# Gated attention block on one core: the second batch's transposed input by DMA and GpSimd, and the first batch's GELU low parts ahead of quantising W1

## The reference

```python
xn = layernorm(x)
q, k, v = (gelu(xn @ W1 + b1) @ W2 + b2 for each of q, k, v)
scores = tril(q @ k.T / sqrt(256 * 512))
s = layernorm(scores @ v) * ln_w + ln_b
Wq1, Wq2 = quantise(W1), quantise(W2)
h = relu(xn @ Wq1.T + b1)
g = silu(h @ Wq2.T + b2)
out = x + s * g
```

## Time and profile before

| | |
|---|---|
| median of 3 runs | 307.65 us |
| profiled execution, its own time | 307.09 us |
| span of its instructions | 305.4 us |
| PE busy | 299.8 us, 98% |
| VectorE (DVE) busy | 247.6 us, 81% |
| ScalarE (ACT) busy | 222.4 us, 73% |
| GpSimd (POOL) busy | 133.7 us, 44% |
| granted TensorE clock, mean | 0.999 |
| DMA | 19.06 MB, mean 62 GB/s |

### The profile page before, as it was taken

The page is one execution under the profiler, slowest core; times in us unless marked ns, Lnnn a source line. Parts: engine busy times, 40 slices in busy tenths (PEclk is TensorE's granted clock), DMA queues, the critical chain, the costliest instruction groups (busy, mean ns, idle before and its releaser), DMA issues.

```text
span 305.4 us, 5730 instructions
## 1 busy us (share of the span) xinstructions
PE 299.8 (98%) x1856; PEld 268.7 (88%) x1856; DVE 247.6 (81%) x546; ACT 222.4 (73%) x429; POOL 133.7 (44%) x105
## 2 busy tenths in 40 slices
PE   8999999999999999999999999999999999999995
PEld 7878899889988899888997889888998889988895
DVE  4989798967999589976999669995799858696686
ACT  3696948966786857949489576877679494895862
POOL 3945835167060942429151580609515291404200
PEclk9999999999999999999999999999999999999999
DMA  7970044510007000240004200070001500020001
GB/s 235 375 217 2 1 140 137 166 43 2 1 2 206 0 0 0 58 149 0 0 0 143 64 0 0 1 206 1 0 0 32 174 0 0 0 71 2 0 2 69
DMA packets 15228, 19.06 MB, mean 62 GB/s; under 512 B 1776, under 2 KB 12528, under 8 KB 15216
## 3 DMA queue, kind: packets, MB, share of 16 engines
q1 hardware_dynamic: 14656, 18.51, 19.2%
q10 hardware_dynamic: 560, 0.40, 0.4%
HBM read 14.69 MB, written 4.22 MB: 62 GB/s over the span
## 4 chain that ended last, share of the span: by engine, by line
PE 89%; DVE 4%; DMA 3%; SPq 2%; ACT 1%; issue 0%; POOL 0%; DVEq 0%
PE bank L860 87%; DMA x_all<-in_w1t 3%; DVE g L666 1%; SPq L201 1%; DVE gw L780 1%; DVE gw L658 1%; DVE x_all L660 0%; PE bank L974 0%; DVE gw L809 0%; PE bank L975 0%; DVE w1q L611 0%; ACT r_lo L408 0%; PE bank L972 0%; SPq L212 0%; PE bank L844 0%
## 5 line engine op out<-in xcount | busy, mean ns | idle before, releaser
L756 DVE TENSOR_TENSOR r_lo<-bank,r_hi 128x512 fp32r<-128x512 f32 x64 | 44.0, 691 | 34.8 <-ACT bank L471 34.6
L470 ACT ACTIVATE r_hi<-bank,col 128x512 fp32r<-128x512 f32 x64 | 47.0, 734 | 24.6 <-PE bank L860 24.6
L471 ACT ACTIVATE bank<-bank,col 128x512 f32<-128x512 f32 x64 | 45.4, 710 | 0.0
L367 POOL TENSOR_TENSOR o_rstd<-o_var,neg_half 128x2 f32<-128x2 f32 x16 | 11.2, 699 | 76.2 <-ACT o_var L504 76.2
L322 POOL TENSOR_TENSOR y<-y,xn 128x512 f32<-128x512 f32 x12 | 19.7, 1643 | 56.4 <-DMA y<-in_x_t 56.4
L860 PE MATMUL bank<-xT_lo,w1q 128*128 128x512 f32 x128 | 39.5, 390 | 0.0
L860 PE MATMUL bank<-xT_hi,w1q 128*128 128x512 f32 x128 | 39.5, 390 | 0.0
L449 ACT ACTIVATE g<-bank,col 128x512 fp32r<-128x512 f32 x48 | 34.3, 714 | 1.0 <-PE bank L860 0.9
L860 PE MATMUL bank<-w2q,r_lo 128*128 128x256 f32 x256 | 34.6, 278 | 0.0
L860 PE MATMUL bank<-w2q,r_hi 128*128 128x256 f32 x256 | 34.3, 276 | 0.0
L450 ACT ACTIVATE bank<-bank,col 128x512 f32<-128x512 f32 x48 | 33.1, 689 | 0.0
(11 more groups left out here) (150 smaller groups left out, 686.5 us busy)
## 6 DMA issues: line engine op xcount, KB each, us to landing
out<-x_all SPq DMA_DIRECT2D x15, 256.0 KB, 3.1
x_all<-in_x SPq DMA_DIRECT2D x7, 512.0 KB, 3.5
xn<-x_norm_rows SPq DMA_DIRECT2D x6, 512.0 KB, 4.2
y<-in_x_t SPq DMA_DIRECT2D x6, 512.0 KB, 4.8
x_all<-in_w1t SPq DMA_DIRECT2D x2, 512.0 KB, 7.8
x_all<-in_w2t SPq DMA_DIRECT2D x1, 1024.0 KB, 10.4
row<-in_rows SPq DMA_DIRECT2D x1, 512.0 KB, 4.7
x_all<-in_x SPq DMA_DIRECT2D x1, 256.0 KB, 3.2
```

Source lines behind the costliest of these rows:

```text
L367: nc.gpsimd.tensor_tensor(o_rstd[:, half], o_var[:, half], neg_half[:, half], ALU.pow).then_inc(o_rstd_made, 1)
L470: nc.scalar.activation(r["hi"][:, f], pre[:], ACT.Relu, bias=b1)
L471: nc.scalar.activation(pre[:], pre[:], ACT.Relu, bias=b1).then_inc(f1_whole, 1)
L756: nc.vector.tensor_tensor(r["lo"][:, f], bank[(AT_F1 + f) % BANKS][:], r["hi"][:, f].bitcast(FP32), ALU.subtract).then_inc(r_split, 1)
```

## The change

Batch 1's transposed input is made as that of the later batches. SP's queue issues `load_xT(1)` and `spread_x_norm(1)` right behind the bias rows and before the loads of x 2 and x 3; the wait on `x_norm_stored` is now for the batch's own store. `xn1_tile`, the two tiles on VectorE and the eight transposes are gone. GpSimd's part of batch 0 has a new order: the parts of e first, then the bias row, both `xT_centre`, `quantise_rest` and both `xT_scale`. It starts when all six `g_lo` are made, and `quantise_rest` waits for VectorE's third flags pass in place of the finished `quantise2`. VectorE makes `g_lo` 2 to 5 ahead of `quantise1(0)`; `thresholds(0)` stands between `g_lo` 3 and 4, and `thresholds(1)` behind `quantise1(1)`. ScalarE and VectorE make batch 1's xT parts at the place of the later batches, behind the score parts.

```diff
             def batch(i, first=False, second_last=False, last=False):
                 if first:
-                    pool.wait_ge(x_rstd_made, 1)
-                    pool.wait_ge(xT_summed, 2 * CK)
-                    pool.wait_ge(w1_quantized, 1)
-                    xn1_tile(0)
-                    xn1_tile(1)
-                    pool.wait_ge(v_shift_made, CK + 1)
-                    nc.gpsimd.tensor_scalar(row[:, ROW_B2V], row[:, ROW_B2V], v_shift[:, CK:CK + 1], None,
-                                            ALU.add).then_inc(v_centred, 1)
+                    pool.wait_ge(g_split, 6)
                     pool.wait_ge(e_made, 1)
...
-                    pool.wait_ge(w2_quantized, 1)
+                    pool.wait_ge(v_shift_made, CK + 1)
+                    nc.gpsimd.tensor_scalar(row[:, ROW_B2V], row[:, ROW_B2V], v_shift[:, CK:CK + 1], None,
+                                            ALU.add).then_inc(v_centred, 1)
+                    pool.wait_ge(xT_loaded, 16)
+                    pool.wait_ge(x_norm_loaded, 16)
+                    for k in range(CK):
+                        xT_centre(k)
+                    pool.wait_ge(flags_made, 3)
                     quantise_rest()
+                    for k in range(CK):
+                        xT_scale(1, k)
...
@@ vector engine
+                g_lo(2)
+                g_lo(3)
                 if first:
                     thresholds(0)
+                g_lo(4)
+                g_lo(5)
+                if first:
                     dve.wait_ge(thr_made, 2)
                     quantise1(0)
-                g_lo(2)
-                g_lo(3)
-                g_lo(4)
-                g_lo(5)
-                if first:
                     dve.wait_ge(w1_quantized, 1)
                     quantise1(1)
+                    thresholds(1)
                     dve.wait_ge(w1_quantized, 2)
...
                 if first:
-                    thresholds(1)
                     dve.wait_ge(e_split, 1)
                     quantise2()
...
@@ sync engine
+            load_xT(1)
+            sp.wait_ge(xT_summed, 2 * CK)
+            spread_x_norm(1)
             for b in range(2, RAW1):
                 sp.wait_ge(x_loaded, 16 * b - 16)
                 load_x(b)
...
@@ tensor engine
-                if first:
-                    pe.wait_ge(s_read, TT)
-                    pe.wait_ge(y_read, 1)
-                    transpose_x(xn1_made, [(AT_X1 + k) % BANKS for k in range(CK)], range(TT))
                 ffn_out(i, AT_Y2, (3,), begun=last)
```

More of the change, by code:

```diff
@@ L27 @@
 ORDER = (2, 3, 0, 1, 4, 5)
-AT_X0, AT_X1 = ((2, 3), (4, 6)), 30
+AT_X0 = ((2, 3), (4, 6))
 S_COLS = [T - j * P for j in range(TT)]
@@ L149, in gated_block @@
         x1_stats_made = sem("x1_stats_made")
-        b2q_beside, wq_hi_made, wq_split, wv_hi_made, wv_split, bias_read, xn1_made = (
+        b2q_beside, wq_hi_made, wq_split, wv_hi_made, wv_split, bias_read = (
             sem("b2q_beside"), sem("wq_hi_made"), sem("wq_split"), sem("wv_hi_made"), sem("wv_split"),
-            sem("bias_read"), sem("xn1_made"))
+            sem("bias_read"))
         less_made, more_made, w2_rest_quantized = sem("less_made"), sem("more_made"), sem("w2_rest_quantized")
@@ L223, in spread_x_norm @@
                 sp.dma_start(x_norm_rows[b], x_norm[:]).then_inc(x_norm_stored, 16)
-                sp.wait_ge(x_norm_stored, 16 * b - 16)
+                sp.wait_ge(x_norm_stored, 16 * b)
                 sp.dma_start(x_norm_all, x_norm_rows[b].rearrange("(o p) n t -> o (p n t)", o=1).broadcast_to((P, 2 * T))
                              ).then_inc(x_norm_loaded, 16)
+            load_xT(1)
+            sp.wait_ge(xT_summed, 2 * CK)
+            spread_x_norm(1)
             for b in range(2, RAW1):
@@ L242, in store @@
                              x_all[:, b, t:t + tiles]).then_inc(stored, 16)
-            sp.wait_ge(xT_summed, 3 * CK)
             with sp.Fori(1, B - 1) as i:
@@ L302, in _ @@
                                     ALU.subtract).then_inc(w2v_split, 1)
-            def xn1_tile(t):
-                nc.gpsimd.tensor_scalar(xn[:, t], x_all[:, 1, t], x_mean[:, t:t + 1], x_rstd[:, t:t + 1],
-                                        ALU.subtract, ALU.mult).then_inc(xn1_made, 1)
             def quantise_rest():
@@ L326, in xT_scale @@
                 half = xT32[:, k].rearrange("q (t p) -> q t p", t=TT)
-                pool.wait_ge(xT_centred, CK * (b - 2) + k + 1)
+                pool.wait_ge(xT_centred, CK * (b - 1) + k + 1)
                 nc.gpsimd.tensor_tensor(half, half, x_rstd_all, ALU.mult).then_inc(xT_normalised, 1)
@@ L344, in batch @@
                                             ALU.subtract).then_inc(e_split, 1)
-                    pool.wait_ge(w2_quantized, 1)
+                    pool.wait_ge(v_shift_made, CK + 1)
[6 more added lines that the diff above has]
+                    pool.wait_ge(flags_made, 3)
                     quantise_rest()
+                    for k in range(CK):
+                        xT_scale(1, k)
                 elif not last:
-                    pool.wait_ge(xT_loaded, 16 * i)
-                    pool.wait_ge(x_norm_loaded, 16 * i)
+                    pool.wait_ge(xT_loaded, 16 * i + 16)
+                    pool.wait_ge(x_norm_loaded, 16 * i + 16)
                     for k in range(CK):
@@ L424, in xT_hi @@
                 for k in range(CK):
-                    act.wait_ge(xT_normalised, CK * (b - 2) + k + 1)
+                    act.wait_ge(xT_normalised, CK * (b - 1) + k + 1)
                     nc.scalar.copy(xT["hi"][:, k], xT32[:, k]).then_inc(xT_hi_made, 1)
@@ L488, in batch @@
                     nc.scalar.copy(s["hi"][:, at], s32[:, at]).then_inc(s_hi_made, 1)
-                if not (first or last):
+                if not last:
                     xT_hi(i + 1)
@@ L516, in batch @@
                 squares(1)
-                if first:
-                    for k in range(CK):
-                        act.wait_ge(xT_summed, 2 * CK + k + 1)
-                        nc.scalar.copy(xT["hi"][:, k], bank[(AT_X1 + k) % BANKS][:]).then_inc(xT_hi_made, 1)
                 if not last:
@@ L569, in x_statistics @@
                     return
-                dve.wait_ge(xn1_made, TT)
-                dve.wait_ge(x_norm_stored, 16 * b - 32)
+                dve.wait_ge(x_norm_stored, 16 * b - 16)
                 for t in range(TT):
@@ L704, in batch @@
                 if first:
+                    dve.wait_ge(thr_made, 2)
+                    quantise1(0)
                     dve.wait_ge(w1_quantized, 1)
                     quantise1(1)
+                    thresholds(1)
                     dve.wait_ge(w1_quantized, 2)
@@ L791, in batch @@
                 if not last:
-                    if not first:
-                        xT_lo(i + 1, [xT32[:, k] for k in range(CK)])
-                        dve.wait_ge(xT_split, 2 * i + CK + 4)
+                    xT_lo(i + 1, [xT32[:, k] for k in range(CK)])
+                    dve.wait_ge(xT_split, 2 * i + CK + 4)
                     y_bias(AT_Y0, 0, 2, 3 * i + 1)
@@ L799, in batch @@
                     o_scale(0)
-                    if first:
-                        xT_lo(1, [bank[(AT_X1 + k) % BANKS][:] for k in range(CK)])
                     y_bias(AT_Y2, 3, 1, 3 * i + 3)
```

2 lines of the change are left out of this document (removed).

## The result

The changed kernel takes 309.93 us, the median of 4 runs (309.22 to 310.64), against 307.7 us in 4 runs of the kernel before on the same chip (307.64 to 307.9). The ratio is 1.0067, 95% interval 1.0046 to 1.0088: slower, and inside the forecast's range. A second measurement of the same code gave 309.77 us (6 runs), ratio 1.0051 [1.0034, 1.0068].

What follows compares the result with a forecast made beforehand. TensorE, busy 98% of the span, was taken as the bound. V -0.8, Y0 +1.85, O +0.85, transposes -0.87, batch 1 +0.6 gave +1.6 us: 307.09 to 308.7 profiled, 309.25 as median; range 305.9 to 310.3.

Steps and rivals of the forecast that it cites:

- Transposes: Step 1, TensorE in batch 0: the eight transposes go, all on the path, a gain of 0.87 us.
- V: Step 2, V of batch 0: starts at 22.5 instead of 23.29 us without its wait, gain 0.8 us.
- Exclusion: Step 3, VectorE against GpSimd in batch 0: passes wait for each other, Y0 starts at 38.8, 1.05 us later than before.
- the short hold of the `tensor_scalar`: Within step 3: a GpSimd `tensor_scalar` lets go of VectorE's two-input pass about 0.3 us after it gets in.
- O: Step 4, O of batch 0: waits for GpSimd's low part of v, starts at 45.1, 1.9 us later than before.
- Batch 1: Step 5, start of batch 1: O's 1.9 us less the transposes' 0.87, so 1.03 us late.
- Wait at V: Step 6, V of batch 1: `g_lo` end at 62.0, V is wanted at 61.4, another 0.6 us lost.
- the uncertain holds: Bounds in batch 0: `tensor_scalar` holds of 0.3 us or all of it, the latter +0.5 us.
- the whole gain: Rival for batch 0: passes keep quiet lengths, Y0 and O just in time, -0.8 - 0.87, 306.0 us; chance 0.15.
- full holds: Rival: GpSimd's `tensor_scalar` passes shut out VectorE's L611 to their end, all behind 0.5 us later, 309.8 us; chance 0.15.
- late transfers: Rival: mean and 1/std reach GpSimd at 28 instead of 26.6 us, all behind 0.4 later, 309.7 us; chance 0.06.
- About no change: Rival: GpSimd gets in first behind flags 2 with a short hold, no wait in batch 1, 307.5 us; chance 0.14.

## Why the prediction was right, step by step

The forecast was 1.6 us over before; the medians say 2.2 and 1.8, the starts of V of batch 1 say 1.5 in both traces. By its steps, with the times of the second trace (0.2 earlier as a whole):

| step | forecast | measured |
|---|---|---|
| 2: V of batch 0, no wait | 22.5 | 22.28 |
| 3: e_lo ends | 25.3 | 25.08 |
| 3: second quantising pass ends | 27.2 | 27.05 |
| 3: third flags pass ends | 30.95 | 30.81 |
| 3: last piece of W2 ends, Y0 | 38.8 | 38.66, 38.91 |
| 4: low part of v ends, O | 45.05, 45.1 | 44.96, 45.01 |
| 6: V of batch 1 | 61.95 | 61.64, after a wait of 0.25 |

1. **Transposes.** The gain of 0.87 is there: from O, 1.8 behind before, to the start of batch 1 (50.33, against the 49.4 of before) the lag shrinks by it.
2. **V.** Right in both traces.
3. **Exclusion.** Right to 0.1 us once the start is taken off. That VectorE would get in first behind the third flags pass was right too, and so was the short hold of the `tensor_scalar`: with a hold to its end, the second quantising pass would have ended 0.5 later. What this step left out is D: it waits 0.54 us for an `r_lo`. It costs nothing, since Y0 waits for GpSimd anyway.
4. **O.** Right; the pass that waited longest is the 128x128 multiply, 2.10 us.
5. **Batch 1.** 0.95 late at its start, 1.2 with the earlier start of this execution counted; the sum had 1.03.
6. **Wait at V.** The forecast was 0.6; the traces list 0.25 and none. By the starts, V follows the pair ahead of it by 0.87 and 0.68 us in place of 0.45, so 0.4 and 0.2 us are lost. The term was too large: `g_lo` ends at 59.04 + 2.48 = 61.52, 61.7 with the start counted, not 62.0. The run with the statistics moved (0.74) and the one with batch 0 free of waits (0.78) show that this wait is real and grows when VectorE comes late out of batch 0, or TensorE early.

What remains between 1.5 and the medians' 1.8 to 2.2 is not in batch 0. From 66 to 305 us the groups of TensorE's feed-forward products with the quantised W2 are, in the kernel before:

```profile
L860 PE MATMUL bank<-w2q,r_lo 128*128 128x256 f32 x224 | 30.2, 277 | 0.0
L860 PE MATMUL bank<-w2q,r_hi 128*128 128x256 f32 x224 | 29.9, 276 | 0.0
```

and in the second trace of the changed one:

```profile
L847 PE MATMUL bank<-w2q,r_lo 128*128 128x256 f32 x224 | 30.7, 280 | 0.0
L847 PE MATMUL bank<-w2q,r_hi 128*128 128x256 f32 x224 | 30.5, 279 | 0.0
```

The same 448 products are busy for 1.1 us more, without a wait. But in the changed kernel with the statistics moved they take 61.1 us and in the one with batch 0 free of waits 60.1, and this part of the span also differed between the other kernels, whose code there is the same: 245.0 to 246.0 us. Whether the change has a hand in it stays open. The range held since it took in such errors by the uncertain holds, not because I had named this one.

Of the rivals, the whole gain is out by the waits, full holds by the row at 25.67, late transfers by GpSimd, which never waited for them. "About no change" is what the version without waits in batch 0 reached (1.0014), with another order.

## What to carry to other kernels

Before work is moved off the busiest engine, ask when the engine that takes it will run, and beside which passes: here a saving of 0.87 us of TensorE put 6.6 us on GpSimd, in place of 2.45, at the one time when VectorE's string fed the next product, and each meeting cost the one the rest of the other. Write the passes of both engines as one queue, start plus duration, with a rule for who gets in first; this gave the starts to within 0.3 us blind. When a step is moved on one engine, go through what the other engine starts from it: in the kernel before, with `g_lo` first and nothing else, GpSimd's string began later and its end fell on passes of VectorE that had been quiet (4.17 us for 0.73), and the run came out 2.7 us slower than expected. The longest wait in the list, for a threshold, hid behind a later one and by the trace cost nothing: ask of each wait what the next product would wait for without it.

## What the runs showed of the hardware

- Two GpSimd memsets of 1.17 us each do not delay VectorE's two-input pass (0.69 us beside the second); a GpSimd pass with two SBUF inputs does, until it ends (2.54 in place of 0.55).
- A VectorE `tensor_scalar` from SBUF to SBUF waits in the same way: two of 128x256, 0.41 us each in the kernel before, took 1.78 and 2.47 beside GpSimd's `tensor_tensor` passes, and ended 0.16 and 0.15 us after them (the order of VectorE alone, in the kernel before).
- A GpSimd `tensor_scalar` holds VectorE's two-input pass up only a little: 1.38 us for 1.28, although GpSimd's pass went on until 26.44 (second trace of the changed kernel), and 1.46 for 1.28 beside GpSimd's xn tiles, 24.44 to 27.62 (same run as above).
- The 34 warm-up products, the same code each time, took between 5.44 and 7.00 us in 13 profiled executions, and what follows shifts with them: the last pair of K in batch 0 starts between 21.83 and 22.86. The first product that has no wait tells how much of a difference is only that.
- From V of batch 1 to the end, the span differed by up to 1.5 us between executions (245.0 to 246.5) with a mean granted clock of 0.998 to 1.000. For a change worth under 0.5%, one profile does not give the sum. The start of one product in the stage that changed says what that stage did, but not the median either: it stood 0.1 us behind the kernel before where the median was 1.0 above (without the four passes), and 0.4 ahead where the median was 0.3 above (no waits in batch 0).
